# A state-space scan on one Trainium2 core: VectorE's products with C, two per step over two PSUM banks each instead of four over one

## The reference

```python
h = x * rsqrt(mean(x * x) + EPS) * norm_scale
xs, res = split(h @ w_in)                      # 512 channels each
res = silu(res)
xs = silu(causal_depthwise_conv(xs, conv_w) + conv_b)
delta, B, C = split(xs @ w_xproj)              # 16, 16 and 16 columns
delta = softplus(delta @ w_dt + b_dt)
deltaA = exp(delta[..., None] * A)             # per channel and state
deltaBx = (delta * xs)[..., None] * B
ys = scan over time: h[t] = deltaA[t] * h[t-1] + deltaBx[t]
y = sum over the states of ys * C
out = (y + xs * D) * res
return x + out @ w_out
```

## Time and profile before

| | us |
|---|---|
| median of 3 runs | 2117.26 (2116.98 to 2119.85) |
| the profiled execution, its own time | 2117.91 |
| its span, first to last instruction | 2116.2 |
| TensorE busy in the span | 1649.7 |
| VectorE busy | 1322.9 |
| ScalarE busy | 892.7 |
| GpSimd busy | 862.8 |

### The profile page before, as it was taken

The page is one execution under the profiler, slowest core; times in us unless marked ns, Lnnn a source line. Parts: engine busy times, 40 slices in busy tenths (PEclk is TensorE's granted clock), DMA queues, the critical chain, the costliest instruction groups (busy, mean ns, idle before and its releaser), DMA issues.

```text
span 2116.2 us, 20605 instructions
## 1 busy us (share of the span) xinstructions
PE 1649.7 (78%) x5491; PEld 813.7 (38%) x5492; DVE 1322.9 (63%) x1984; ACT 892.7 (42%) x1598; POOL 862.8 (41%) x399
## 2 busy tenths in 40 slices
PE   6386886868777686876766999949999999999800
PEld 2121221313122131220114677626767676766600
DVE  3298998989999898998983443323333333333345
ACT  4577566766567656674422334302222212121200
POOL 0677868577685857868621212200000000000065
PEclk9697988979999798988997999979999999999955
DMA  4633435344552643425309101111010101010034
GB/s 125 149 81 91 108 74 134 74 102 96 121 119 46 142 90 93 110 60 140 80 0 369 63 27 40 40 49 34 30 35 30 35 30 35 30 35 30 27 114 124
DMA packets 105433, 169.86 MB, mean 80 GB/s; under 512 B 14624, under 2 KB 53264, under 8 KB 105248
## 3 DMA queue, kind: packets, MB, share of 16 engines
q1 hardware_dynamic: 99232, 152.44, 28.1%
q0 software_dynamic: 6144, 16.79, 2.5%
HBM read 127.76 MB, written 41.42 MB: 80 GB/s over the span
## 4 chain that ended last, share of the span: by engine, by line
PE 42%; DVE 28%; ACT 8%; issue 7%; POOL 7%; DMA 5%; SPq 1%; another core or an unknown queue 0%; DVEq 0%; POOLq 0%; ACTq 0%
DVE psH L915 19%; PE psA L1401 12%; PE psP L1418 12%; DVE X L924 6%; PE psP L1326 5%; PE psH L1335 5%; PE psH L1409 3%; DMA ud_dram<-ud 3%; POOL X L416 2%; PE psP L1251 2%; ACT psH L761 1%; POOL gat L469 1%; ACT L761 1%; POOL ud L404 1%; POOL ud L401 1%
## 5 line engine op out<-in xcount | busy, mean ns | idle before, releaser
L416 POOL TENSOR_TENSOR X<-rep,B 128x2048 f32<-128x2048 f32 x128 | 577.9, 4526 | 210.9 <-PE psA L1281 179.7
L1281 PE MATMUL psA<-X,gsum 128*32 128x512 f32 x1024 | 366.5, 668 | 188.0 <-DVE X L924 187.7
L761 ACT ACTIVATE psH<-rep,A_q 128x512 f32<-128x512 f32 x512 | 352.5, 690 | 171.8 <-DVE X L924 162.8
L915 DVE TENSOR_TENSOR_SCAN psH<-psH,X 128x512 f32<-128x512 f32 x256 | 313.0, 1223 | 96.0 <-POOL X L416 49.0
L915 DVE TENSOR_TENSOR_SCAN psH<-psH,carry,X 128x512 f32<-128x512 f32 x256 | 331.2, 1294 | 30.6 <-ACT psH L761 30.5
L924 DVE TENSOR_TENSOR X<-psH,C 128x512 f32<-128x512 f32 x512 | 349.5, 683 | 0.0
L469 POOL DMA_INDIRECT gat<-eo_dram,slots x64 | 62.2, 972 | 667.7 <-DVE slots L1158 645.7
L1401 PE MATMUL psA<-ew_s,nTb 128*128 x576 | 268.3, 609 | 0.8 <-ACT nTb L836 0.8
L1418 PE MATMUL psP<-ew_s,hT 128*128 x1152 | 262.2, 381 | 2.6 <-ACT hT L842 2.6
L1418 PEld LDWEIGHTS psP<-ew_s,hT 128*128 128x128 f32 x1152 | 220.0, 191 | 63.4 <-issue 36.8
L1281 PEld LDWEIGHTS psA<-X,gsum 128*32 128x32 f32 x1024 | 49.1, 113 | 496.4 <-DVE X L924 443.6
(11 more groups left out here) (172 smaller groups left out, 1619.9 us busy)
## 6 DMA issues: line engine op xcount, KB each, us to landing
rep<-ud_dram SPq DMA_DIRECT2D x128, 512.0 KB, 8.7
ud_dram<-ud SPq DMA_DIRECT2D x32, 512.0 KB, 8.8
ew_s<-in_L_ffn_ew_dram SPq DMA_DIRECT2D x16, 1024.0 KB
xb<-rows_dram SPq DMA_DIRECT2D x72, 128.0 KB, 2.0
eo_dram<-eo SPq DMA_DIRECT2D x72, 128.0 KB, 1.7
B<-bc_dram SPq DMA_DIRECT2D x128, 64.0 KB, 3.9
C<-bc_dram SPq DMA_DIRECT2D x128, 64.0 KB, 4.5
out_dram<-fin SPq DMA_DIRECT2D x8, 512.0 KB
```

The source lines that it names most:

```text
L416: nc.gpsimd.tensor_tensor(X[:, Q % NX], rep[:, g % 2, 1], B4[:, f:f + 1, :].broadcast_to([P, NR, TC]), ALU.mult).then_inc(bx_ready, 1)
L761: nc.scalar.activation(psH[:, r, :], rep[:, g % 2, 0, r, :], ACT.Exp, scale=A_q[:, c, r, f:f + 1]).then_inc(dA_ready, 1)
L915: nc.vector.tensor_tensor_scan(psH[:, r, :], psH[:, r, :], X[:, Q % NX, r, :], start, ALU.mult, ALU.add).then_inc(scan_done, 1)
L1281: ins = nc.tensor.matmul(psA[r * GJ:(r + 1) * GJ, g % 2, :], gsum[:], X[:, Q % NX, r, :], start=False, stop=(f == NF - 1), skip_group_chec ...
```

## The change

The product of a step is done for two banks at once: `output_pair(Q, r)` reads psH[r:r + 2] (two PSUM banks, 128x1024), multiplies by C4[f] broadcast over both, writes X[r:r + 2] and counts `hc_ready` up by 2. `products(Q, r)` now gives the count at which the pair that holds r is done, so the exponentials of banks 0 and 1 of the next step both wait for one pair, those of banks 2 and 3 for the other, and so do the summing matmuls and `load_c`. VectorE's order in a step becomes s0, P23 of the step before, s1, s2, P01, s3. The number of scans, what is computed and the other engines' programs stay as they are.

```diff
--- before.py
+++ after.py
@@ -352,7 +352,7 @@
 
         def products(Q, r):
 
-            return Q * NR + r + 1
+            return Q * NR + r - r % 2 + 2
 
         def summed(Q):
 
@@ -915,14 +915,14 @@
                 nc.vector.tensor_tensor_scan(psH[:, r, :], psH[:, r, :], X[:, Q % NX, r, :], start,
                                              ALU.mult, ALU.add).then_inc(scan_done, 1)
 
-            def output_step(Q, r):
+            def output_pair(Q, r):
 
                 f = Q % NF
                 if Q % NQ < NF:
                     dve.wait_ge(c_here[f], 64 * (Q // NQ + 1))
-                dve.wait_ge(scan_done, Q * NR + r + 1)
-                nc.vector.tensor_tensor(X[:, Q % NX, r, :], psH[:, r, :], C4[:, f, :],
-                                        ALU.mult).then_inc(hc_ready, 1)
+                dve.wait_ge(scan_done, Q * NR + r + 2)
+                nc.vector.tensor_tensor(X[:, Q % NX, r:r + 2, :], psH[:, r:r + 2, :],
+                                        C4[:, f:f + 1, :].broadcast_to([P, 2, TC]), ALU.mult).then_inc(hc_ready, 2)
 
             def gate(k, c):
                 g = k * CH + c
@@ -944,15 +944,14 @@
                 for q in range(NQ):
                     scan(k, q, 0)
                     if k or q:
-                        output_step(k * NQ + q - 1, 3)
+                        output_pair(k * NQ + q - 1, 2)
                     scan(k, q, 1)
-                    output_step(k * NQ + q, 0)
                     if q == 7:
                         gate(k, 0)
                     if k and q == OUT_AT + 1:
                         residual(k - 1, 0)
                     scan(k, q, 2)
-                    output_step(k * NQ + q, 1)
+                    output_pair(k * NQ + q, 0)
                     if k and q == 2:
                         gate(k - 1, 3)
                     if q == 10:
@@ -960,10 +959,9 @@
                     if q == 14:
                         gate(k, 2)
                     scan(k, q, 3)
-                    output_step(k * NQ + q, 2)
                     if k and q == OUT_AT + 1:
                         residual(k - 1, 1)
-            output_step(NT * NQ - 1, 3)
+            output_pair(NT * NQ - 1, 2)
             gate(NT - 1, 3)
             for j in range(2):
                 residual(NT - 1, j)
```

## The result

The changed kernel takes 2133.86 us (median of 4 runs, 2132.60 to 2135.52) against 2117.59 for the kernel before beside it: ratio 1.0075, 95% interval 1.0058 to 1.0093. It is 16.3 us slower; 18 were forecast. The last product ends at 1115.90 us instead of 1099.97, so 15.9 us of it lie in the state-space stage; behind it the two profiles differ by 0.5 us (1015.66 against 1016.19).

A forecast was written before the change was run, and what follows sets the result against it. VectorE was taken to set the pace in the state-space stage, inside a closed loop with ScalarE, TensorE and GpSimd. Tiles 1 to 6 +13.8, tile 0 +3.0, tile 7 +1.45 sum to 18.25 us: 2135.3 us, range 2121 to 2150.

The forecast's parts named there:

- Leg 1: VectorE without a stall, bank 2's scan in step 14 to the product before the SiLUs: 60.02 us, +1.4 (odd +1.5).
- Legs 2 and 3: ScalarE's SiLUs until bank 3's scan in step 7, unchanged 8.05 us; then VectorE until step 8's first residual, -0.64.
- Leg 4: Step 8's first residual to bank 3's scan in step 9, through TensorE's x projection: 10.43 us, no change (odd +0.1).
- Leg 5: Bank 3's scan in step 9 to bank 2's in step 14: 43.31 us, +1.45 in its first part.
- 5b: Logarithm's table load to bank 2's scan in step 14, through GpSimd and the store of ud: 35.2 us, unchanged.
- The loop: Five legs closing one tile's time, 127.0 us: +2.2 even, +2.4 odd, 13.8 over tiles 1 to 6.
- leg 5a: Bank 3's scan in step 9 to the logarithm's table load on ScalarE: 9.56 against 8.11 us, +1.45.
- The end tiles: First and last tile of the state-space stage: tile 0 loses 3.0 us, tile 7 loses 1.45.
- Rival 4: SyncE's queue: a late product holds the load of C and thus the second store of ud: 2149 us, chance 0.04.
- rival 3: Plain steps lack the 0.08 us to spare: 2146 us, or 2150 if a tail is not overlapped; chance 0.11.
- rival 1: ScalarE's lost lead costs nothing, only the pairs' 12.8 us gain shows: 2105 us, chance 0.12.
- Rival 2: A pair on VectorE is cheaper than 1.13 us: 2121 us at 0.14 saved; chance 0.07.

The follow-up runs named there:

- e8: Kernel before with ScalarE's second softplus group one step later and GpSimd's input chunks 2 and 3 behind steps 2 and 3: 2065.86 us against 2117.56, ratio 0.9751.
- e1: Changed kernel with each pair done as two single-bank products, new order and grouped waits kept: 2142.07 us against 2112.33 for the kernel before, ratio 1.0139.
- e2: As e1, but each exponential and summing matmul waits for its own bank, so only VectorE's order differs from the kernel before: 2128.41 us against 2112.33, ratio 1.0077.
- e9: Changed kernel with the later softplus group and GpSimd's input chunks 2 and 3 later: 2078.63 us against 2117.56 for the kernel before, ratio 0.9809.
- e10: e8 with ScalarE's long jobs out (SiLUs on one element, a copy for the logarithm): 2020.23 us against 2117.56 for the kernel before, ratio 0.9537.
- e11: e9 with ScalarE's long jobs out (SiLUs on one element, a copy for the logarithm): 2012.89 us against 2117.56 for the kernel before, ratio 0.9503.
- e3: Changed kernel with each two-bank product directly behind its second scan: 2139.91 us against 2112.33 for the kernel before, ratio 1.0129.
- e5: Changed kernel with ScalarE's second softplus group one step later: 2110.29 us against 2112.16 for the kernel before, ratio 0.9991.
- e7: e5 with ScalarE's long jobs out (SiLUs on one element, a copy for the logarithm): 2042.68 us beside 2112.16 for the kernel before.
- e4: Kernel before with ScalarE's second softplus group one step later: 2089.31 us against 2112.16, ratio 0.9893.
- e6: e4 with ScalarE's long jobs out (SiLUs on one element, a copy for the logarithm): 2036.54 us beside 2112.16 for the kernel before.

## Why the prediction was right, point by point

- *The instructions.* 0.05 us a pair was taken; 0.05 to 0.06 was measured (1.13 against 1.18 or 1.19). The recorded duration was 1206 ns for a forecast 1225.
- *Leg 1.* +1.4 us forecast, +1.2 in tile 4 (odd: 61.37 to 62.6, +1.2 for +1.5). A half step of two scans and a pair takes 3.37 us on average in plain even steps, where 3.39 was put in.
- *Legs 2 and 3.* 8.05 and -0.64 forecast, 8.04 and -0.65 measured, with the stall of 3 us at gate 0 and 0.85 at s3(7).
- *Leg 4.* No change forecast in even tiles (+0.1 in odd ones), -0.26 measured in tile 4. The term left out TensorE's granted clock: 0.68 over the projection before, 1.00 after. In tile 5 it was 0.54 before, and the leg 11.5 us before and 10.5 after, 1.0 less. That the clock was higher there after the change was luck and no part of the prediction.
- *Leg 5.* +1.45 forecast, +1.42 measured; 5b unchanged at 35.3. The new stall at s2(11), 2.05 us, is covered by the wait for GpSimd at s3(13), as said.
- *The loop.* Tiles 1 to 6 lost 11.3 us for a forecast 13.8. Of the 2.5 us between them leg 4 makes 1.5, leg 1 1.3, leg 5a 0.3 and leg 3 0.1; leg 5b, which was 0.7 longer, takes some back.
- *The end tiles.* Tile 0 gave +4.15 for a forecast 3.0, tile 7 +0.4 for 1.45, and the two errors cancel. That is luck: 1.2 us of tile 0 is a later first scan (86.5 instead of 85.3), which the change does not explain, since the first scan comes at 86.4 in e8 with its single products and at 85.0 in e1. Without it the stage would have lost 14.7 us for the forecast 18.25.
- *The queues.* SyncE's load of C stood ahead of the second store of ud without delaying it: that store was issued 22.05 us behind the logarithm's table load in tile 4, before and after. Rival 4 did not happen, nor rival 3 (no gaps in plain steps), nor rival 1: e1, e2 and the sign change between e8/e9 and e10/e11 show that the lead does cost. Rival 2 was tried by e1: the wide product gives 0.06 us, not 0.14.
- *VectorE's idle time.* Some 50 us more were forecast; by the page it is 824.4 us (2131.6 - 1307.2) against 793.3, 31 more. The forecast took 36 us off the busy time from recorded durations, but 0.1 us of each product's tail had lain under the next scan already; the busy time fell by 15.7. The sum did not rest on it.
- *The Trainium skill's two rules.* The Trainium skill (Perfetto Trace Analysis, "Optimizing Scalar/DVE Operations") says that grouping can improve throughput if the engine is saturated; e10 and e11 agree, where VectorE is idle 1.3 and 6.7 us in the whole stage and the pairs win 7.3. It also says that an engine which is not saturated but causes bubbles elsewhere may be better broken up into smaller instructions; the kernel as it is agrees in the sign. But the size of the instruction is not what costs: by itself it won 13.4 us (e1 against the changed kernel). What costs is what its consumers then wait for.

## What to carry to other kernels

Grouping two instructions saves their fixed cost once, and takes from whoever waits for the first of them the time of all that now stands in between: price both, the second at every place where the waiting engine has a long job. Plain steps hide it (here 0.08 us to spare sufficed); the jobs of several microseconds, a SiLU or a logarithm with its table loads, pay it in full. Look at the order apart from the size: here the new order alone cost as much as the whole change (e2). And where a tile's time is a closed loop through several engines, find the wait that closes it first: moving that (e8) gave 52 us, seven times what the pairs can win in the best case seen here.

## What the runs showed of the hardware

- A product that waits for the scan right in front of it on VectorE starts 0.14 us behind that scan's end, against 0.1 us before it when one other instruction stands between: 0.2 us and more for each such wait (e3), several times what the grouping of two products gives back.
- The granted clock of TensorE in the stage fell from 0.89 to 0.75 with the same matmuls, when the sums of two banks at a time came together; it was 0.84 in e2, where each waits for its own bank. TensorE's two levels are 1.2 and 2.4 GHz. The same split holds in all kernels run: 0.75 to 0.78 in those with grouped waits (the changed kernel, e1, e3, e5, e7, e9, e11), 0.84 to 0.96 in those where each sum waits for its own bank (before, e2, e4, e6, e8, e10). Of the five legs only the fourth goes through TensorE, and there the changed kernel happened to be granted more, so no cost of it shows here. Why the arrival of the sums moves the level was not separated further.
